# Chunk maxima by a matrix product, row checks split over two steps, and layer 0's weights prepared in the first tiles

## The reference, cut to what matters

```
layer 0: w = einsum('nd,dkio->nkio', emb, weight)      # N=2048, D=16, K=3, 64x64
         x_g = [x, A x, (2 A A - I) x];  f = sum over k, i of x_g * w  + emb @ bias
layer 1: attention with mask adj > 0.5, softmax, elu
layer 2: (adj + I) @ (x W^T + b) / rowsum
layer 3: v = x with row 0 replaced;  three times:
         h = relu([v, adj v] W1^T + b1);  v = h W2^T + b2
```

## Time and profile before

| | us |
|---|---|
| median of 3 runs (1138.82 to 1142.53) | 1139.39 |
| the profiled execution | 1138.65 |
| its span (first to last instruction) | 1136.8 |
| TensorE busy in the span | 1062.6 (93%) |
| VectorE, ScalarE, GpSimd busy | 677.1, 389.5, 472.9 |

### The profile page before, as it was taken

How to read it: one execution, slowest core, us unless ns; L and a number is a source line. 1 busy time by engine, 2 the same in 40 slices (tenths; PEclk the granted TensorE clock), 3 DMA queues, 4 the chain that set the end, 5 groups by cost and what they waited for, 6 DMA issues and landing times.

```text
span 1136.8 us, 18591 instructions
## 1 busy us (share of the span) xinstructions
PE 1062.6 (93%) x7044; PEld 508.3 (45%) x7044; DVE 677.1 (60%) x1760; ACT 389.5 (34%) x851; POOL 472.9 (42%) x571
## 2 busy tenths in 40 slices
PE   8969999999999999999999889938999999999994
PEld 3425444434434443443455445524545454455542
DVE  4965665676557766766656767735454554336566
ACT  3342233334344444344225444425334411112111
POOL 2203586646358666856714241324323224322110
PEclk9979999999999999999999999978999999999997
DMA  9650000000000000000101111101112100001101
GB/s 370 237 219 1 1 2 1 1 1 2 1 1 2 1 1 2 1 1 1 38 1 59 54 46 67 38 37 37 41 71 74 38 2 1 3 1 32 35 28 56
DMA packets 14656, 45.64 MB, mean 40 GB/s; under 512 B 961, under 2 KB 9281, under 8 KB 10081
## 3 DMA queue, kind: packets, MB, share of 16 engines
q1 hardware_dynamic: 14560, 44.39, 10.7%
HBM read 40.19 MB, written 4.19 MB: 39 GB/s over the span
## 4 chain that ended last, share of the span: by engine, by line
PE 66%; DVE 17%; issue 6%; ACT 4%; DMA 3%; POOL 3%; SPq 0%; ACTq 0%; POOLq 0%; DVEq 0%
PE PS L512 39%; PE PS L641 20%; DMA R<-at_in 3%; DVE X L878 2%; DVE S L878 2%; DVE T L878 2%; ACT WZ L767 2%; DVE ra L881 2%; DVE T L881 1%; DVE R L878 1%; ACT T L767 1%; DVE X L1162 1%; PE PS L503 1%; PE PS L504 1%; PE PS L505 1%
## 5 line engine op out<-in xcount | busy, mean ns | idle before, releaser
L512 PE MATMUL PS<-Bm,S 128*128 128x512 f16 x2816 | 636.2, 382 | 13.4 <-DVE T L878 9.8
L512 PEld LDWEIGHTS PS<-Bm,S 128*128 128x128 f16 x2816 | 270.2, 98 | 338.0 <-issue 24.1
L641 PE MATMUL PS<-WZ,R 64*128 64x512 f16 x1536 | 198.5, 377 | 3.2 <-ACT T L767 3.2
L767 ACT ACTIVATE T<-PS,SM 128x128 f32<-128x128 f32 x384 | 112.8, 366 | 205.9 <-DVE X L878 137.5
L1354 POOL TENSOR_TENSOR T<-T 128x128 f32<-128x128 f32 (+1 forms) x192 | 127.4, 664 | 124.5 <-ACT T L767 114.1
L1354 POOL TENSOR_TENSOR T<-R,T 128x512 f16<-128x512 f32 x48 | 55.8, 1162 | 215.0 <-DVE T L1193 172.4
L878 DVE SCALAR_TENSOR_TENSOR X<-PS,SM,X 128x128 f32<-128x128 f32 x320 | 109.4, 342 | 38.8 <-PE PS L641 38.4
L641 PEld LDWEIGHTS PS<-WZ,R 64*128 64x128 f16 x1536 | 69.2, 94 | 106.9 <-issue 25.4
L1193 DVE CAST T<-R 128x512 f16<-128x512 f32 x48 | 24.5, 511 | 137.7 <-ACT R L767 137.7
L641 PE MATMUL PS<-WZ,T 64*128 64x512 f16 x768 | 103.8, 376 | 0.0
L878 DVE SCALAR_TENSOR_TENSOR T<-PS,SM,T 128x128 f32<-128x128 f32 x256 | 87.6, 342 | 20.5 <-PE PS L641 20.5
(11 more groups left out here) (192 smaller groups left out, 1188.6 us busy)
## 6 DMA issues: line engine op xcount, KB each, us to landing
WZ<-a_in SPq DMA_DIRECT2D x16, 1024.0 KB, 4.8
R<-at_in SPq DMA_DIRECT2D x15, 1024.0 KB, 7.4
out<-X SPq DMA_DIRECT2D x16, 256.0 KB, 2.3
X<-x_in SPq DMA_DIRECT2D x3, 1024.0 KB, 15.8
T<-w_in SPq DMA_DIRECT2D x1, 1536.0 KB, 15.8
R<-at_in SPq DMA_DIRECT2D x2, 512.0 KB, 5.1
SM<-sm_in SPq DMA_DIRECT2D x1, 520.5 KB, 15.8
X<-x_in SPq DMA_DIRECT2D x2, 256.0 KB, 4.8
```

Of the source, the lines that this page charges most:

```text
L512: m = e.matmul(o, stile(h, t, c), Bm[:, t, block(j)], start=(t == 0 and h == 0), stop=(last and t == NT - 1 and h == 1))
L641: m = e.matmul(bank(b0 + q), halves[kd][zh][r, :], WZ[r, wh, kd, block(g)], start=(i == 0), stop=(i == 8))
L767: return e.activation(o, i, f, **kw)
```

## The change

- The maximum over the partitions in `gmax`/`step` is taken by a product: the column `gmh` of 128 per-partition maxima, now fp16, is repeated over 128 columns and multiplied with the identity (`gcol`, a new small product on TensorE in the same five banks), so that each partition holds all 128 maxima in a row; VectorE takes the maximum of that row. `gmax` and `step` stand one place earlier.
- The row check is cut in two: `chk` keeps VectorE's row maximum and ScalarE's sum of `Bm`, which waits for nothing of the check; ScalarE's sum of signs becomes `sgn`, one place later. The next tile of `adj` is still fetched when the sign is done.
- `V0T` is made by one VectorE instruction (`v0t`, one place before `v0`) from constants prepared in `rows`; GpSimd has no part in it.
- `w0` is fetched before x's third group and pair 1. VectorE makes the difference and the means at jt 3 and subtracts them at jt 4; ScalarE takes a sum of squares (jt 5), GpSimd spreads its maximum, ScalarE takes the root (jt 10) and the high half (jt 11), VectorE the low half (jt 12). The doubling is folded into the scale of E2 (2/EDGE for 1/EDGE). The scale of x is 16 for 32.

```
-SX = 32.0
+SX = 16.0
...
+cRow0, cRest = 34, 35
...
-HEAD = ([("R", jt) for jt in range(4)] + [("wz",)] + [("R", jt) for jt in range(4, 9)] + [("wlo",)]
-        + [("R", jt) for jt in range(9, 13)]
+HEAD = ([("R", jt) for jt in range(13)]
...
-        at(k + 1, ("rs", 2, c), ("apply", 2, c, 0), ("apply", 2, c, 1))
+        at(k + 1, ("rs", 2, c), ("apply", 2, c, 0), ("apply", 2, c, 1), ("v0t", c))
...
-            at(16 * p + 4 * c + 5, ("gmax", p, c))
-            at(16 * p + 4 * c + 6, ("step", p, c))
+            at(16 * p + 4 * c + 4, ("gmax", p, c))
+            at(16 * p + 4 * c + 5, ("gcol", p, c), ("step", p, c))
...
         at(6 + 2 * it, ("chk", it))
+        at(7 + 2 * it, ("sgn", it))
...
+                    elif kind == "gcol":
+                        done = (s_gmr, 4 * (step[1] - 1) + step[2] + 1)
...
             tiles_of_x(1)
+            e.dma_start(w0, w0_in).then_inc(s_w0, 16)
             tiles_of_x(2)
             pair(1)
             tiles_of_x(3)
             pair(2)
-            e.dma_start(w0, w0_in).then_inc(s_w0, 16)
             pair(3)
...
+                    p, c = step[1:]
+                    o = pe_aux(e, step)
+                    e.wait_ge(s_gmx, 4 * (p - 1) + c + 1)
+                    e.matmul(o[:, 0:128], gmh[:, c:c + 1].broadcast_to([128, 128]), i16[:, :], start=True,
+                             stop=True).then_inc(s_gmc, 1)
...
+                if jt == 5:
+                    e.wait_ge(s_wb, 1)
+                    fn(WZ[:, 1, :, :].rearrange("p k n -> p (k n)"), w0, ACT.Square, accum_out=wst[:, 0:1]).then_inc(s_wsq, 1)
+                elif jt == 10:
+                    e.wait_ge(s_wsqr, 1)
+                    fn(col(cT3), col(cT3), ACT.Sqrt).then_inc(s_wroot, 1)
+                elif jt == 11:
+                    e.wait_ge(s_wz, 1)
+                    fn(WZ[:, 0, :, :].rearrange("p k n -> p (k n)"), w0, ACT.Copy, scale=col(cZ)).then_inc(s_whi, 1)
...
                 elif kind == "chk":
                     it = step[1]
+                    e.wait_ge(s_zp, 8 * NT)
+                    if it:
+                        e.wait_ge(s_cnt, it)
+                    fn(junk, Bm[:, it, :], ACT.Copy, accum_out=cnt[:, it:it + 1]).then_inc(s_cnt, 1)
+                elif kind == "sgn":
+                    it = step[1]
                     e.wait_ge(s_nr, it + 1)
                     if it:
                         e.wait_ge(s_sign, it)
-                        e.wait_ge(s_cnt, it)
                     fn(rowt, rowt, ACT.Sign, bias=nr[:, it:it + 1], accum_out=sg1[:, it:it + 1]).then_inc(s_sign, 1)
-                    fn(junk, Bm[:, it, :], ACT.Copy, accum_out=cnt[:, it:it + 1]).then_inc(s_cnt, 1)
...
-                elif jt == 10:
-                    e.wait_ge(s_wa, 2)
+                elif jt == 3:
+
+                    e.wait_ge(s_w0, 16)
+                    vc(e.tensor_tensor(w0[:, 0:1024], w0[:, 0:1024], w0[:, 2048:3072], ALU.subtract))
                     vc(red(e, wsum[:, 0:48], w48, ALU.add))
-                    ts(e, wsum[:, 0:48], wsum[:, 0:48], -1.0 / C, None, ALU.mult).then_inc(s_wmean, 1)
+                    vc(ts(e, wsum[:, 0:48], wsum[:, 0:48], -1.0 / C, None, ALU.mult))
+                elif jt == 4:
+                    e.tensor_tensor(w48, w48, wsum[:, 0:48].unsqueeze(2).broadcast_to([128, 48, C]), ALU.add).then_inc(s_wb, 1)
+                elif jt == 11:
+                    e.wait_ge(s_wroot, 1)
+                    vc(ts(e, col(cZ), col(cT3), 1e-30, 1.0 / 1024, ALU.max, ALU.mult))
+                    vc(ts(e, col(cEz), col(cZ), 1.0 / SX, None, ALU.mult))
+                    e.reciprocal(col(cZ), col(cZ)).then_inc(s_wz, 1)
+                elif jt == 12:
+                    e.wait_ge(s_whi, 1)
+                    stt(e, WZ[:, 1, :, :].rearrange("p k n -> p (k n)"), w0, col(cZ),
+                        WZ[:, 0, :, :].rearrange("p k n -> p (k n)"), ALU.mult, ALU.subtract).then_inc(s_wlo, 1)
...
-                elif jt == 14:
-                    e.wait_ge(s_wb, 1)
-                    red(e, wst[:, 0:1], w0, ALU.max, True).then_inc(s_wmax, 1)
...
-                    e.wait_ge(s_wmaxr, 1)
-                    vc(ts(e, col(cZ), col(cT3), 1e-30, 1.0 / 1024, ALU.max, ALU.mult))
-                    vc(ts(e, col(cEz), col(cZ), 1.0 / SX, None, ALU.mult))
-                    e.reciprocal(col(cZ), col(cZ)).then_inc(s_wz, 1)
-                elif kind == "wlo":
-                    e.wait_ge(s_whi, 1)
-                    stt(e, WZ[:, 1, :, :].rearrange("p k n -> p (k n)"), w0, col(cZ),
-                        WZ[:, 0, :, :].rearrange("p k n -> p (k n)"), ALU.mult, ALU.subtract).then_inc(s_wlo, 1)
...
+                elif kind == "v0t":
+                    c = step[1]
+                    e.wait_ge(s_n[2], 4 * c + 1)
+                    if c:
+                        e.wait_ge(s_vh, 4 * c - 3)
+                        e.wait_ge(s_vl, 4 * c - 3)
+                    stt(e, V0T, X[:, 0, chunk(c)], col(cRest), ROWI, ALU.mult, ALU.add).then_inc(s_vt, 1)
...
-                    red(e, gmr[:, c, 0:1], gm[:, c, :], ALU.max).then_inc(s_gmx, 1)
+                    red(e, gmh[:, c:c + 1], gm[:, c, :], ALU.max).then_inc(s_gmx, 1)
...
-                    e.wait_ge(s_gmr, 4 * (p - 1) + c + 1)
-                    fc(e.tensor_tensor(col(cT0), gmr[:, c, 1:2], iG, ALU.mult))
+                    n = 4 * (p - 1) + c + 1
+                    e.wait_ge(s_gmc, n)
+                    red(e, gmr[:, c:c + 1], bank(aux_bank["gcol", p, c])[:, 0:128], ALU.max).then_inc(s_gmr, 1)
+                    e.wait_ge(s_gmr, n)
+                    fc(e.tensor_tensor(col(cT0), gmr[:, c:c + 1], iG, ALU.mult))
...
-            e.tensor_tensor(w0[:, 0:1024], w0[:, 0:1024], w0[:, 2048:3072], ALU.subtract).then_inc(s_wa, 1)
-            e.wait_ge(s_wa, 1)
-            ts(e, w0[:, 2048:3072], w0[:, 2048:3072], 2.0, None, ALU.mult).then_inc(s_wa, 1)
-            e.wait_ge(s_wmean, 1)
-            w48 = w0.rearrange("p (g o) -> p g o", o=C)
-            e.tensor_tensor(w48, w48, wsum[:, 0:48].unsqueeze(2).broadcast_to([128, 48, C]), ALU.add).then_inc(s_wb, 1)
-            e.wait_ge(s_wmax, 1)
-            e.partition_all_reduce(col(cT3), wst[:, 0:1], 128, RED.max).then_inc(s_wmaxr, 1)
+            e.wait_ge(s_wsq, 1)
+            e.partition_all_reduce(col(cT3), wst[:, 0:1], 128, RED.max).then_inc(s_wsqr, 1)
...
-                elif kind == "v0" and step[2] == 0:
-                    c = step[1]
-                    e.wait_ge(s_n[2], 4 * c + 1)
-                    if c:
-                        e.wait_ge(s_vl, 4 * c - 3)
-                    e.tensor_copy(V0T, X[:, 0, chunk(c)]).then_inc(s_vt, 1)
-                    e.wait_ge(s_vt, 2 * c + 1)
-                    ts(e, grid(V0T[0:1, :]), rows[0:1, 2:3, :].broadcast_to([1, 2, C]), LAM, None, ALU.mult).then_inc(s_vt, 1)
...
-                elif kind == "gmax":
-                    p, c = step[1:]
-                    e.wait_ge(s_gmx, 4 * (p - 1) + c + 1)
-                    e.partition_all_reduce(gmr[:, c, 1:2], gmr[:, c, 0:1], 128, RED.max).then_inc(s_gmr, 1)
```

More of the change, by code:

```diff
@@ L205, in gnn_kernel @@
         xm = sb("xm", [128, NT], F32)
-        gm = sb("gm", [128, NC, 4], F32)
-        gmr = sb("gmr", [128, NC, 2], F32)
+        gm = sb("gm", [128, NC, 4], F16)
+        gmh = sb("gmh", [128, NC], F16)
+        gmr = sb("gmr", [128, NC], F32)
         wst = sb("wst", [128, 2], F32)
@@ L227, in gnn_kernel @@
         s_xa = sem("s_xa")
-        s_wa, s_wmean, s_wb, s_wmax, s_wmaxr, s_wz, s_whi, s_wlo = (
-            sem(f"s_{k}") for k in ("wa", "wmean", "wb", "wmax", "wmaxr", "wz", "whi", "wlo"))
+        s_wb, s_wsq, s_wsqr, s_wroot, s_wz, s_whi, s_wlo = (
+            sem(f"s_{k}") for k in ("wb", "wsq", "wsqr", "wroot", "wz", "whi", "wlo"))
         s_p1, s_u1h, s_u1, s_nr, s_sign, s_q, s_dg = (
@@ L250, in gnn_kernel @@
         s_g, s_ut, s_uh, s_ul = (sem(f"s_{k}") for k in ("g", "ut", "uh", "ul"))
-        s_gt, s_gh, s_gl, s_gm, s_gmx, s_gmr, s_kg = (
-            sem(f"s_{k}") for k in ("gt", "gh", "gl", "gm", "gmx", "gmr", "kg"))
+        s_gt, s_gh, s_gl, s_gm, s_gmx, s_gmc, s_gmr, s_kg = (
+            sem(f"s_{k}") for k in ("gt", "gh", "gl", "gm", "gmx", "gmc", "gmr", "kg"))
         s_f, s_y3, s_fin = (sem(f"s_{k}") for k in ("f", "y3", "fin"))
@@ L306, in gnn_kernel @@
         V0T = flatR[:, 3072:3200]
+        ROWI = flatR[:, 4544:4672]
         SQ = [T3[:, 512:1024]]
@@ L746, in act_e2 @@
                 e.wait_ge(s_zp, 8 * (u - 2))
-            e.activation(U2[:, u % 3, 0, :], bank(0), ACT.Copy, scale=1.0 / EDGE).then_inc(s_u2h, 1)
+            e.activation(U2[:, u % 3, 0, :], bank(0), ACT.Copy, scale=2.0 / EDGE).then_inc(s_u2h, 1)
         def act_dx(e, u):
@@ L841, in scalar_steps @@
                     if j == 0:
-                        e.wait_ge(s_vt, 2 * c + 2)
+                        e.wait_ge(s_vt, c + 1)
                         e.wait_ge(s_sc, 1)
@@ L881, in red, with lo_half @@
```

(11 more changed lines are left out.)

7 lines of the change are left out of this document (1 added, 6 removed).

## The result

The changed kernel takes 1095.80 us (median of four runs, 1095.47 to 1097.06) against 1139.95 (1138.82 to 1142.53) for the kernel before: a ratio of 0.9612, 95% interval 0.9593 to 0.9630. The profiled execution took 1095.81 us, its span is 1094.0 us (before 1136.8). So 42.8 us are gone between the two profiled executions.

The account below looks back on a forecast made before the run. TensorE, busy 93% of the span, was taken as the bound, losing time to waits and slow clock. Waits -33.1, clock -5.5, late wait -1.2, head -1.0, matmuls +0.5, residue +2.0 gave -38.3: 1101 us, range 1094 to 1112.

Parts of the forecast that it names:

- the likeliest case: Whole kernel: the change works as forecast and the time lands at 1095 to 1106 us; chance 0.69.
- Waits, clock and the late wait of the tail: TensorE, 600 to 800 us: six waits go, -33.1, and half-clock time, -5.5; one wait late in the tail, -1.2.
- Residue of 2.0: Tail row checks: TensorE time kept for later requests of the next tile and late signs, +2.0 us, bounds 0 and 12.
- new matmuls of 0.5: TensorE in the tail: the eight small products that replace the reductions add 0.5 us, bounds 0.4 and 5.
- the sign comes 3 us later, and VectorE waits some 2 us: Checks at k = 21, 25, 29, 33, sharing a place with `step`: VectorE waits some 2 us, inside TensorE's bank slack.
- The head: Start of the kernel, up to the first product: the reordered weight work gains little, -1.0 us, bounds -4 and +3.
- Behind it the ring's DMAs set the pace both times: Head after tile 15: DMA landings set the pace, so taking 3.41 us out of VectorE there gives little.
- Only the reduction was the bound: Rival, tail: VectorE stays late from its own work, the check's waits stay, 17.5 us; time 1119, chance 0.07.
- GpSimd stays late: Rival, tail: the 7.31 us behind the reduction belong to following work, about 7 us of wait stay; 1108, chance 0.04.
- DMA takes the place of the wait: Rival, row checks: landings take 7 us, VectorE waits 1.5 to 3.5 us at each of 16; 1110, chance 0.14.
- Slower, TensorE waits for `gmh`: Rival, new small products: VectorE's maximum comes too late at all eight and TensorE waits in its order; 1142, chance 0.02.
- VectorE's idle time before `T<-R` down to under 1: Sign of success at the row checks: VectorE's idle time before these evictions falls from 4.5 us to under 1.

Follow-up runs that it names:

- late sign: Changed kernel with ScalarE's sum of signs another place later, so each next row tile is asked for later still; 1104.30 us, ratio 0.9690.
- the next experiment: Changed kernel with the weights' high half after ScalarE's last tile and the low half in three pieces between second-half tiles; 1088.77 us, ratio 0.9557.
- the version without them: Kernel with the halves of WZ after the tiles, plus w0 fetched after pair 1 and x's second group, means and squares later; 1086.33 us, ratio 0.9517.

## Why the prediction was right, and which terms were mis-sized

The forecast of 1101 with 1094 to 1112 held: 1095.8, at the early end of the likeliest case (1095 to 1106).

*Waits, clock and the late wait of the tail* (33.1 + 5.5 + 1.2 = 39.8 us): right. The waits went, 33.0 us by the windows and 1.2 us near the end. With the head's 2.6 us, and 0.3 us that a wait near 935 us grew, 6.2 of the 42.8 us between the two profiled executions are left for the clock, the new matmuls' own time taken off; I had 5.5 for the clock. So the sum of -38.3 lay 4.5 us short: 2.0 of residue and 0.5 of matmuls that didn't show, 1.6 us of the head, 0.7 us of clock, less the 0.3. No two large errors cancelled in it.

*Residue of 2.0 and new matmuls of 0.5*: both too large. TensorE waits nowhere for the tiles of `adj` or for `gmh`; what the eight matmuls take themselves can't be told apart in the 42.8 us. The step that failed is "the sign comes 3 us later, and VectorE waits some 2 us" where `step` stands in the same place. VectorE waited once, for 0.51 us, because it no longer comes that early to its row maximum. The late sign shows what an actual delay costs: 73.1 us of VectorE's waits became 8.5 us of time. The cover of the new matmul, forecast as 4.5 us to spare, was 1.9 us at its least.

*The head*, -1.0: mis-sized, -2.6 by the trace and -2.9 by the run of it alone (by that run's own trace -1.9 up to 530 us). Tile 15 was not "at the same time within 1 us" but 1.6 us earlier. The bound of -4, "the low half's whole price", was the better guess: the next experiment, which takes that pass out from among the tiles, moved tile 15 by another 6.5 us and the first product by 5.2. "Behind it the ring's DMAs set the pace both times" was wrong as a limit: the whole ring follows tile 15, for a pair is fetched only when VectorE has freed its buffer. TensorE's waits at tiles 2 to 6 cost nothing while 4.80 us of waiting stood at the end, as I had it. Once that wait was gone, the version without them was 2.4 us faster (1088.77 to 1086.33), of which the traces don't show all to be theirs.

*How the sum splits between the causes*: this is where my working was off, though not the sum. I gave the check 14.3 + 3.2 = 17.5 us. Alone it brings 27.7, and undoing it in the changed kernel costs 24.9. I gave the reduction with V0T 14.26 + 4.54 + 1.2 + 2.3 of clock, 22.3 us. They bring 17.5 alone, and, by subtraction, 1112.14 - 1095.8 - 2.9 = 13.4 us behind the split check. The step that failed is the plain attribution of a wait to its last releaser: the 14.26 us ended with V0T behind the reduction, but the chain of 19.5 us began only 5.3 us before TensorE ran out of work. With the split check it began 16.4 us before. The second reason is the clock. I took its price from the three slow products of the earlier trace rows, and without the split check the same kind of wait made five products slow, up to 10.6 us in place of 3.2. The time of the whole change was safe against this error, because it takes all six waits away, whosever they are; a forecast of a part was not (1122.5 for the check alone, measured 1112.14).

*The rivals.* "Only the reduction was the bound" is out: the check is the larger part. "GpSimd stays late" is out in the changed kernel (its trace has no idle time of 7 us on GpSimd in this stretch that waits for nothing shown), and the reduction's row in the kernels that keep it shows the gap behind it each time: 6.80, 8.61 and 7.61 us. The Trainium skill, GPSIMD Engine Reference, calls GpSimd in its introduction the correct choice for cross-partition reductions. By the runs it is a harmless one only while nothing waits for GpSimd: 2.3 us for eight in one version, 13.2 in another. The same page of the Trainium skill has about 6 us in section 2.1 for the first call of a freshly loaded routine. Here it was 5.82 to 6.15 us ahead of each of the eight calls of the kernel before, not of the first alone, and 6.74 to 7.38 us stood behind each. "DMA takes the place of the wait" was not met, and has its price in the experiment with the late sign. "Slower, TensorE waits for `gmh`" appeared as 2.32 us there, and as 1.54 us at 731.79 with the product alone, both where VectorE was late; in the changed kernel 1.9 us of cover or more stood before it.

*What I had said would show*: no reduction but that of `flags`, TensorE busy for all of 600 to 760, clock 1.00: so it was. "VectorE's idle time before `T<-R` down to under 1" was not: it is 2.58 us in the row above, because ScalarE itself waits there, 0.72 us, for TensorE's product, which is what an engine that has caught up looks like. The first product came at 71.60, before the 72 to 73 given; TensorE's last wait of the head was 4.80, not 6.

What stays open is why a wait of 1.94 us was followed by a product of 8.76 us in one kernel, while one of 3.60 us was followed by 7.07 us in another, and by 7.76 and 9.44 us in two more (last section). No run was made for it.

## What to carry to other kernels

A wait names the releaser that came last, not the price of removing it. Two causes that meet in one wait share it, so take each out alone and also each alone out of the changed kernel; here the parts alone summed to 48.1 us (27.7 + 17.5 + 2.9) and together gave 44.2. Taken out of the changed kernel one at a time, the check cost 24.9 us, the product 2.3 and the move of V0T nothing.

If a step on a shared engine waits for another engine ahead of an eviction that a third one needs (here the sum of signs), move the waiting step behind the eviction before speeding up anything else.

In a prologue, work on the engine that frees a ring's buffers delays every later transfer. Put it where that engine waits for the ring.
